# Products that nobody reads, added on TensorE in both halves of a two-layer kernel

## What is computed

```
for layer in (0, 1):
    xn = layernorm(x)
    s = attention(xn)   # 0: windows of 10 and 20 tokens, then a dense gelu FFN; 1: all 512 tokens, 16 heads of 8
    g = experts(xn)     # 8 experts, the top 2 of each token; layer 0 has a shared expert too
    x = x + s * silu(g)
```

## Time and profile before

| | |
|---|---|
| median of 3 runs | 1742.53 us (1740.51 to 1747.9) |
| the profiled execution, its own time | 1744.1 us |
| its span | 1742.3 us |
| busy: TensorE, VectorE, ScalarE, GpSimd | 67%, 64%, 39%, 26% |

### The profile page before, as it was taken

How to read it: one execution, slowest core, us unless ns; L and a number is a source line. 1 busy time by engine, 2 the same in 40 slices (tenths; PEclk the granted TensorE clock), 3 DMA queues, 4 the chain that set the end, 5 groups by cost and what they waited for, 6 DMA issues and landing times.

```text
span 1742.3 us, 17058 instructions
## 1 busy us (share of the span) xinstructions
PE 1167.2 (67%) x5494; PEld 630.5 (36%) x5494; DVE 1111.4 (64%) x1856; ACT 684.7 (39%) x1166; POOL 453.8 (26%) x412
## 2 busy tenths in 40 slices
PE   4464665757585765532456647699997778787886
PEld 4332333434343432311122222288882323232331
DVE  3566758585857657215577586466667878677761
ACT  1112333333323333120223436443445766656663
POOL 2156611120202111243444147500003303213110
PEclk9967868777777868555556769599998888788885
DMA  8210212121221110016033124556544333253400
GB/s 281 101 59 27 71 52 67 43 83 33 83 67 58 62 40 29 6 26 81 17 56 50 18 44 98 113 169 200 200 150 74 49 45 55 41 77 45 73 20 7
DMA packets 73726, 125.03 MB, mean 72 GB/s; under 512 B 13541, under 2 KB 31014, under 8 KB 73638
## 3 DMA queue, kind: packets, MB, share of 16 engines
q1 hardware_dynamic: 65446, 107.15, 25.5%
q0 software_dynamic: 8192, 16.79, 4.0%
HBM read 57.74 MB, written 40.37 MB: 56 GB/s over the span
## 4 chain that ended last, share of the span: by engine, by line
PE 42%; DVE 23%; issue 12%; POOL 10%; ACT 8%; DMA 3%; SPq 2%; DVEq 0%; ACTq 0%; POOLq 0%
PE PS L770 5%; PE PS L813 5%; PE PS L673 5%; PE PS L623 4%; POOL XS1D L1163 4%; PE PS L790 4%; PE PS L832 4%; PE PS L573 3%; ACT P L880 3%; PE PS L750 2%; DVE MX L1553 2%; DVE WS L1307 2%; POOL YG L1147 2%; PE PS L578 2%; PE PS L736 2%
## 5 line engine op out<-in xcount | busy, mean ns | idle before, releaser
L1553 DVE TENSOR_REDUCE MX<-PS 128x1 f32<-128x512 f32 x512 | 323.8, 685 | 132.5 <-PE PS L750 123.5
L880 ACT ACTIVATE P<-PS 128x512 f32<-128x512 f32 x512 | 278.0, 596 | 194.8 <-PE PS L790 192.7
L790 PE MATMUL PS<-QS,KS 50*128 50x512 f32 x512 | 138.2, 536 | 103.6 <-ACT P L880 98.1
L750 PE MATMUL PS<-KS,QS 48*128 48x512 f32 x512 | 149.3, 580 | 66.9 <-DVE MX L1553 40.5
L770 PE MATMUL PS<-P,V 128*32 128x512 f32 x1024 | 180.3, 786 | 0.0
L1147 POOL DMA_INDIRECT A<-Y1D,POS x64 | 73.5, 1148 | 281.2 <-DMA Y1D<-YE 190.8
L750 PEld LDWEIGHTS PS<-KS,QS 48*128 48x128 f32 x512 | 58.0, 224 | 218.7 <-DVE MX L1553 112.6
L790 PEld LDWEIGHTS PS<-QS,KS 50*128 50x128 f32 x512 | 60.0, 230 | 165.5 <-ACT P L880 138.8
L623 PE MATMUL PS<-G,HEADSUM 128*128 128x400 f32 (+2 forms) x160 | 81.2, 639 | 51.5 <-DVE WS L1341 50.6
L673 PE MATMUL PS<-XST,WB 128*128 128x512 f32 x184 | 106.2, 732 | 4.4 <-issue 4.4
L813 PE MATMUL PS<-XRH,WH 128*128 128x512 f32 (+1 forms) x276 | 103.1, 414 | 0.2 <-DVE A L1495 0.2
(11 more groups left out here) (208 smaller groups left out, 2222.3 us busy)
## 6 DMA issues: line engine op xcount, KB each, us to landing
WH<-W1SD SPq DMA_DIRECT2D x23, 704.0 KB, 4.3
QS<-EH SPq DMA_DIRECT2D x64, 128.0 KB
KS<-EH SPq DMA_DIRECT2D x64, 128.0 KB
WB<-in_wb SPq DMA_DIRECT2D x23, 322.0 KB, 2.8
XS<-XS0D SPq DMA_DIRECT2D x23, 256.0 KB, 2.7
Y0D<-YE SPq DMA_DIRECT2D x23, 256.0 KB, 2.0
XS<-XS1D SPq DMA_DIRECT2D x23, 256.0 KB, 3.7
Y1D<-YE SPq DMA_DIRECT2D x23, 256.0 KB, 2.7
```

Of the source, the lines that this page charges most:

```text
L750: signal(pe.matmul(PS[:, s % 4, :], QS[rows, u % 3, hp, 128 * t:128 * t + 128], KS[rows, u % 3, hp, :], start=True, stop=True), "ms")
L790: signal(pe.matmul(PS[:, 4 + s % 2, :], KS[rows, u % 3, hp, 128 * k:128 * k + 128], QS[rows, u % 3, hp, :], start=True, stop=True), "st")
L880: act.activation(*a, **k).then_inc(sem[name], 1)
L1553: go("mx", dve.tensor_reduce(MX[:, u % 2, t, 4 * par + hp:4 * par + hp + 1], PS[:, s % 4, :], AX.X, ALU.max))
```

## The change

It adds products whose result is never read: the identity times a 128x512 table, fp32, both in SBUF. In the first half each of slots 3 to 179 of the list ends with two of them into bank 3, except where a pass has had its `pair` and not yet its `gate` (these slots are left out: 147 of 177 remain, 294 products). Ahead of each two stands a wait until VectorE has read bank 3 of the last pass (`lused`). In the second half one stands ahead of each first product of a `max` pair in units 0 to 5, into the bank that the real product then overwrites: 96 products.

```diff
+WARM_UNITS = 6
...
-    for items in slots:
+    for n, items in enumerate(slots):
         out += items
+        if 2 < n < len(slots) - 12:
+            out.append(("warm", 2))
     return out
...
+            def warm(passes, count):
+
+                if passes:
+                    pe.wait_ge(sem["lused"], passes)
+                for _ in range(count):
+                    pe.matmul(PS[:, 3, :], IDENT[:], TRIG[:, 0, :], start=True, stop=True)
+
+            paired = gated = 0
...
                     pair_up(*a)
+                    paired += 1
+                elif what == "gate":
+                    gated += 1
+                elif what == "warm" and gated == paired:
+                    warm(paired, *a)
...
                 if s >= 4 and par == 0:
                     pe.wait_ge(sem["mx"], s - 2)
+                if u < WARM_UNITS and par == 0:
+                    pe.matmul(PS[:, s % 4, :], IDENT[:], TRIG[:, 0, :], start=True, stop=True)
```

## The result

The changed kernel takes 1838.9 us (median of 4 runs, 1837.7 to 1849.7) against 1741.5 in the same series for the kernel before: a ratio of 1.058, 95% interval 1.054 to 1.061. The profiled execution spans 1836.6 us. My prediction was 1783.5, range 1745 to 1826: the direction held, the time lies outside the range.

The account below looks back on a forecast made before the run. TensorE (42%) and VectorE (23%) were taken to lead the chain, with TensorE often at half clock. 1744.1 + 43 (seven batches) - 3 (first batch) + 5 (last tail) - 4 (second half) = 1785; median 1783.5 us, range 1745 to 1826.

Parts of the forecast that it names:

- E: Slots 11 to 13: added pairs wait for the gate and delay L656/658 and VectorE's softmax; +6.6 us a batch.
- the first batch: First half's first batch, which has no tail: only slots 7 to 9 and some of L673 gain; -3 us.
- C: Slot 6: the added pair waits for the gate, so slot 7's sums start later; +1.0 us a batch.
- D: Slots 7 to 9, TensorE and VectorE taking turns: L623 gets faster at full clock; -1.5 us a batch.
- Six batches, 6.2 each: First-half batches with a tail, after the first such one: each longer by the sum of A to E, +6.2 us.
- B: Slots 1 to 5, TensorE alone the chain: faster steps slightly outweigh added products and the gate wait; -0.3 us a batch.
- A: Slots 15 to 0: gate ends earlier, but eight added products and transposes stand before L635; +0.4 us a batch.
- Second half: From X1N through GpSimd's scatters: added products lift the clock and gain slightly; -4 us, bounds -7 to +29.
- The second batch: First batch with a tail: taken to cost the same as the other batches with a tail, +6.2 us.
- The last tail: End of the first half: added products lie ahead of short steps and behind the last L658; +5 us, bounds 0 to 10.
- The third: Rival, clock not held: second half pays +29, B and A lose 3 more a batch; 1837 us, chance 0.12.
- The first rival, the clock wins: First half: products fit TensorE's idle time, full clock saves 10 us a batch; 1672 us, with half 1708; chance 0.14.

Follow-up runs that it names:

- the two partial runs: The change's first-half products alone and its second-half products alone, each against the kernel before, on other chips: ratios 1.042 and 1.011.
- the fastest of the experiments: Kernel before plus full products in slots 3, 7 to 9, 16, 17 of each batch and 128-column products in the last tail, none in the second half: ratio 0.989.

## Why the prediction was wrong

**What was right.** The price of a product (0.86 us, pieces of 0.43), the order of events in E, the first batch (-2.8 for -3), the scatters (64 of them in 84.3 us for 83.9) and the sign. C and D together came to -0.7 for -0.5 (third gate against the sums of slot 6: 31.9 before, 31.2 after).

**The steps that failed,** in order of size. The sum was short by 53 us.

1. **Six batches, 6.2 each for 9.5** (20 off). Three terms share it: B is 1.5 off in the mean, A 1.3, E 0.7, and C with D 0.2 the other way. **B** came to +0.4 in three batches and +2.0 in the other three, for -0.3. I had the pair of slot 3 at full clock, 1.7 us; it took 3.2 to 3.6, in the batch below at a mean clock of 0.59, though TensorE had rested only 1.63 us since L638. (My 1.9 for L635 was its time at half clock; it took 1.05, which hid a part.) The changed kernel, batch from 345.2, and the window of the transposes and the pair:
```profile
357.72 0.62 PE L581 MATMUL PS<-IDENT,XI 128*64 128x128 f32 x4
358.18 3.38 PE L702 MATMUL PS<-TRIG,IDENT 128*128 128x512 f32 x4
361.49 1.73 PE L613 MATMUL PS<-XIT,WQKV 64*32 64x130 f32 x48
```
```profile
357.72:361.49 3.77, 3.77 (x10) 1.33 (x9) 1.38 (x2) 0.84 (x2) 0.00 (x0) 0.59 0.00 0
```
   **A** cost 1.9 to 2.1 in five batches and nothing in the last, for +0.4. I had L673 of slot 15 at full clock and the gate 2.3 us early; L676 took 4.1 to 5.3, and the gate of the batch shown was 0.5 early against the shift. **E** cost 6.6 to 8.3, 7.3 in the mean, for 6.6: I took a start from rest as slow for 4.4 us, with 2.2 lost; in the batch shown all four products ran at nearly half clock and lost 3.2, and L1330 came 8.0 late with the third gate 0.3 early. A does not hang on E alone: without the pairs of slots 11 and 12 L676 took 3.60 and A was +0.4 in two batches, but 4.3 and +2.0 in three; with these pairs behind L661 A was +0.4 to +0.6 in all.
2. **Second half, -4 for +12** (16 off). The step was "I take it that they lift the clock", by which I put the stretch up to the scatters at the favourable end of its bounds. The products did lift it, from 0.57 to 0.69 in the windows above and not beyond the 0.8 that I forecast, and I let the lift pay for everything. 96 products add 46 us to TensorE's busy time up to the scatters (131.7 to 177.4), in a stretch where VectorE's maxima and TensorE's products take turns: L766 alone holds 14.3% of the chain there, 40 us, and GpSimd's gathers (L1147), which held 10.5% before, only 2.7% as L1165. That short products cost next to nothing there fits a price by length. What I had bounded at +29 held it, what I took did not.
3. **The second batch, 6.2 for 20.4** (14 off). I had read one batch and multiplied. Its rows show a gate that ends in time; in the second batch it ends 3.1 us later behind GpSimd's transfers. The wait in slot 2 was priced at 1.6, and there it was 7.0, with 3.6 more lost to slower steps behind it. The run without the pair of slot 2 took 4.6 off that batch on the chips of the experiments, beside 3.8 in each other.
4. **The last tail,** +7.6 for +5, within its bounds (0 to 10).

**My rivals.** The third gave 1837, nearly the time, and that is in part luck: it put +29 on the second half (12 came), and had nothing for the second batch (14 more than forecast). Its 3 a batch on A and B nearly came (2.8 in the six batches), and its core, that the clock is not held, is what happened in B, in A and in the second half. The first rival, the clock wins, failed in this kernel and holds in a small part in the experiments: a higher clock in slots 1 to 5 is worth 3.4 us a batch where no wait is paid for it, a third of the 10 that I had counted from rows.

**Shown:** in the first half 42 of the 65 us between the second L638 and X1N come with the waits alone, and some 50 go when two pairs of products are moved behind the step that they held up (the two overlap). **Open:** why the clock falls in slot 3 and differs at slot 15 between batches of one kernel; and how much of the +12 of the second half is the same on a chip like the first, where the two partial runs were not made.

## What to carry to other kernels

A filler product costs first by what it must wait for, and by what stands behind it in the same queue: bare waits cost 6.9 of 10.1 us a batch here, and the same products behind the urgent step cost almost nothing. Put them behind a wait that has just ended and ahead of one that must come anyway, a few at a time, and let them end before the work that they wake. And when one batch is read for all, look at the first one too: engines that are busy with the start's transfers turn a free wait into a dear one.

## What the runs showed of the hardware

- **The last rest does not tell the clock.** After 3.58 us of rest L694 and L676 took 1.16 and 5.29; in the run without slots 11 and 12, after 3.51 us, 1.16 and 3.60, the same instructions on the same shapes. The rows above show both. In another batch of the changed kernel (from 433.9), again after 3.58 us, they took 2.08 and 4.23.
- **The price of an fp32 product.** In the Trainium skill (TensorE: Matmul & The Clock Gate, Wait — 56ns, not 53.3ns?) a warm product of 512 columns takes 215.7 ns and a cold one 426.7; an fp32 one here shows two pieces of 0.43 us each at full clock, so its whole price is four times the page's warm figure.
- **Short products, two answers.** With 128 columns they brought the sums of slot 6 to 24.6 us (27.1 with none), and left the clock of the second half at 0.58 (0.54 to 0.57 with none).
- **Chips differ beside GpSimd's scatters.** The 64 scatters take 83 to 84 us everywhere. (Each chip was used in one series only, so chip and series can't be told apart.) On the first chip the others work on beside them; on the three of the experiments they nearly stand. The kernel before, then the fastest of the experiments, whose second half is the same code:
```profile
1027.80:1111.70 83.90, 65.47 (x336) 23.88 (x336) 55.14 (x86) 51.73 (x90) 64.69 (x64) 0.81 0.49 110
```
```profile
1017.30:1100.60 83.30, 23.78 (x102) 9.15 (x98) 18.78 (x26) 11.71 (x21) 64.09 (x64) 0.54 0.28 69
```
TensorE is busy 65.5 us in the one and 23.8 in the other, and the core moves 110 and 69 GB/s. The work is made up behind the scatters (24.6 us to the blocks in the one, 89.9 in the other). It is some 65 of the 100 us that these chips are slower by; no run here tells the cause.
